# The router product taken from raw rows during the second layer's maxima, and the expert rows summed in the output tensor

## The chip, the cores and the metric

The kernel runs on one core of one Trainium2 chip. Its engines are PE (TensorE), DVE (VectorE), ACT (ScalarE), POOL (GpSimd) and SP (SyncE), each with its own instruction stream; they meet through semaphores. The metric is the device time of one execution, in microseconds (us), median of several runs; lower is better.

## What is computed

A graph layer of 1250 nodes with 768 features and 21,250 edges, to which a loop for each node is added. In short, with `ln` the layer norm without gain:

```
xn = ln(x)
x1 = x + GNN(xn) + MIX(xn)
GNN: two graph-attention layers (4 heads of 192, then 2 heads of 96, the softmax of each
     node over its edges is taken with the largest score subtracted), result out2 (1250 x 192);
     GNN = [xn, out2] @ Wu + bu
MIX: linear attention with 12 heads, projected
y = ln(x1)
probs = softmax(y @ router_w.T)          # 8 experts, the two most probable of each node are taken
out = x1 + sum over the 2 picks of balanced[t, e] * (silu(y @ w1[e].T) @ w2[e].T)
```

`balanced` divides a probability by a running importance of its expert, computed from the sum of `probs` over all nodes, and scales the two to a sum of one.

## The kernel before

Nodes lie in NT = 10 tiles of P = 128 rows (T = 1280 padded rows). Every engine's program is written out by hand, so its order is the order of the code, and `reserve`/`take`/`finished`/`evacuated` hand the 8 PSUM banks round in a list that all engines share. Before the second attention layer, `acc_d` in DRAM already holds x plus everything of x1 but the out2 part. The parts that matter here, in order of time:

- **First layer's aggregation** (`attention`, `aggregate`): DVE and ACT make one 128 x 1280 score tile per head and source tile, PE multiplies it (L1854). PE starts it after the small product of `b1T`.
- **Second layer's maxima.** PE spreads two columns to rows (`spread_row`, stage `aR`), then DVE runs 20 passes `masked_max` over 128 x 1280 (L1306), ten a head. After each head `leaky_max` gives `ucol`, and PE spreads it (stage `uR2`, L1615 with `ucol`), which ACT copies out (`rows_out`, L967). Only after both heads does ACT enter `attention` of layer 2.
- **Final projection and x1.** `fin_step(t)` on PE turns a tile of out2 and multiplies it by the lower part of Wu (`wuo`, two halves of 384 columns). `residual(t)` on DVE adds it to `x1` and takes the row statistics. SP writes each finished tile of x1 to `sum_d` in DRAM (L596).
- **Router.** For groups of 4, 4 and 2 tiles: `normalized` (DVE) makes y in `yrow`, `y_turned` (PE and ACT) turns it, `logits` (PE) multiplies it by the router weights `rw_raw` (8 columns). `shifted`, `exponentials` and `two_largest` give probabilities and picks, `ranks` (PE) counts places, `places` (DVE) computes the slot of each pick, and POOL scatters the token numbers into `list_d` (L711, two scatters a tile). SP writes y and its gated probabilities to `y_d` (L601).
- **Token lists.** POOL reads `list_d` back (L715). DVE takes from it the token of each of the 128 rows of NS = 27 expert tiles (L1575, 27 passes), into `token_ix`. Rows that no token fills get a padded row's number.
- **Experts** (27 tiles): POOL fetches rows of `y_d` (L721), PE turns them, multiplies by w1, turns, multiplies by w2, ACT and DVE scale by the gate into `yout`, and POOL adds the rows to `sum_d` with an accumulating scatter (L737). Each scatter waits until the one before has landed.
- **End.** When the last scatter has landed, SP copies `sum_d` to `out` in 10 DMAs (L605) and waits for them.

## Time and profile before

| | us |
|---|---|
| median of 3 runs (1143.0 to 1146.82) | 1143.82 |
| time of the profiled execution | 1147.77 |
| its span | 1145.8 |
| PE busy in the span | 958.8 (84%) |
| DVE busy | 679.7 (59%) |
| ACT busy | 404.4 (35%) |
| POOL busy | 406.6 (35%) |

The span runs from the first to the last record of the profiled execution; its own time has 2.0 us more around it. Busy times are averages over stages with different limits, so they don't say what a stage waits for. The chain that ended last is by engine 27% PE, 14% DMA, 12% DVE; its largest DMA piece is the scatter `sum_d<-yout` with 9% of the span.

### The profile page before, as it was taken

Reading aid. Unit: us, or ns where it says so; the run is one execution under the profiler, and the core shown is the slowest. Engines: PE = TensorE matmul, PEld = TensorE weight load, DVE = VectorE, ACT = ScalarE, POOL = GpSimd, SP = SyncE. Lnnn points to the kernel's source line nnn. Section 1 sums busy time; section 2 is a strip of 40 time slices with the busy share of each in tenths; the row PEclk is TensorE's granted clock in tenths of the full one; section 3 lists DMA queues with packets and bytes.
Section 4 is the critical chain, followed back from the end, with each engine's and each line's share of the span. In section 5 each row is a group of like instructions: output and inputs, shape, how many; then the busy total and the mean of one; then the engine's idle time right before and its main releaser. Section 6 shows DMA issues by size and latency. Waiting matters only on the chain.

```text
span 1145.8 us, 14465 instructions
## 1 busy us (share of the span) xinstructions
PE 958.8 (84%) x5152; PEld 815.6 (71%) x5152; DVE 679.7 (59%) x1687; ACT 404.4 (35%) x634; POOL 406.6 (35%) x321
## 2 busy tenths in 40 slices
PE   4999979999999949946999989358797749999991
PEld 3898648676979948946999989257765637767660
DVE  7679997104733215788888867969875362333330
ACT  2543010333320004455778855158421202222220
POOL 3168888888888820002000000000001243443431
PEclk9999997999999988986999989779796559999996
DMA  9986456422544591115000000340261424666556
GB/s 292 218 194 163 73 117 159 83 1 1 111 82 71 129 281 48 25 44 185 28 1 1 1 1 27 112 151 2 96 234 38 170 72 82 127 123 124 115 104 169
DMA packets 76370, 116.14 MB, mean 101 GB/s; under 512 B 33107, under 2 KB 51917, under 8 KB 76141
## 3 DMA queue, kind: packets, MB, share of 16 engines
q0 software_dynamic: 36128, 40.87, 21.2%
q1 hardware_dynamic: 40173, 74.36, 19.9%
q8 instruction: 42, 0.69, 0.2%
q14 instruction: 27, 0.22, 0.1%
HBM read 85.09 MB, written 33.96 MB: 104 GB/s over the span
## 4 chain that ended last, share of the span: by engine, by line
PE 27%; DMA 14%; DVE 12%; issue 5%; ACT 3%; POOL 2%; POOLq 0%; another core or an unknown queue 0%; DVEq 0%; ACTq 0%
PE bank L1615 15%; PE bank L1854 10%; DMA sum_d<-yout,sb_negq 9%; DVE sb_before L1306 5%; DVE pbuf L1361 3%; DMA cnt<-table 3%; DVE pbuf L1372 3%; DMA xs<-y_d,sb_negq 2%; PE bank L1626 2%; ACT h L974 1%; ACT vbuf L988 1%; POOL list_d L711 1%; DVE o L1402 1%; PE bank L1791 1%; ACT pbuf L997 0%
## 5 line engine op out<-in xcount | busy, mean ns | idle before, releaser
L655 POOL DMA_INDIRECT table<-match_n,slot_ix x168 | 278.6, 1658 | 92.9 <-issue 48.4
L1854 PE MATMUL bank<-h,pbuf 128*128 128x193 f32 (+1 forms) x1200 | 191.7, 323 | 20.3 <-DVE pbuf L1372 19.7
L1854 PEld LDWEIGHTS bank<-h,pbuf 128*128 128x128 f32 x1200 | 184.9, 200 | 27.0 <-DVE pbuf L1372 24.4
L711 POOL DMA_INDIRECT list_d<-sb_wk,sb_negq x20 | 19.8, 991 | 342.0 <-DVE sb_negq L1518 336.5
L1306 DVE CUSTOM_DVE_ANT_0 sb_before<-a_row,pen 128x1280 bf16<-128x1280 f32 x60 | 89.5, 1491 | 17.9 <-ACT pen L931 12.5
L1170 DVE SCALAR_TENSOR_TENSOR junk_k<-keyrow,key,sb_before 128x384 uint8<-128x384 f32 x168 | 93.0, 617 | 10.2 <-DMA keyrow<-key_d 9.1
L1615 PE MATMUL bank<-xnT_hi,w_hi 128*128 128x512 f32 (+1 forms) x216 | 85.5, 396 | 11.9 <-issue 8.1
L997 ACT ACTIVATE pbuf<-pbuf 128x1280 f32<-128x1280 f32 x60 | 76.7, 1278 | 42.7 <-DVE pbuf L1361 42.7
L1372 DVE SCALAR_TENSOR_TENSOR pbuf<-pbuf,cnt 128x1280 f32<-128x1280 f32 x60 | 88.8, 1486 | 0.0
L1615 PE MATMUL bank<-w_hi,xnT_hi 128*128 128x384 f32 x240 | 83.1, 346 | 0.0
L1615 PE MATMUL bank<-w_hi,xnT_lo 128*128 128x384 f32 x240 | 81.4, 339 | 0.0
L1615 PE MATMUL bank<-w_lo,xnT_hi 128*128 128x384 f32 x240 | 81.3, 339 | 0.0
L737 POOL DMA_INDIRECT sum_d<-yout,sb_negq x27 | 42.9, 1589 | 106.6 <-DMA sum_d<-yout,sb_negq 73.9
L1615 PE MATMUL bank<-xnT_lo,w_hi 128*128 128x512 f32 (+1 forms) x216 | 78.9, 365 | 0.0
L1615 PE MATMUL bank<-xnT_hi,w_lo 128*128 128x512 f32 (+1 forms) x216 | 78.5, 364 | 0.0
L1615 PE MATMUL bank<-w_all,xT 128*128 x324 | 76.5, 388 | 0.9 <-issue 0.9
L1615 PE MATMUL bank<-w_all,hT 128*128 x216 | 75.3, 492 | 1.5 <-DVE hT L1602 1.5
L1615 PEld LDWEIGHTS bank<-w_all,xT 128*128 128x128 f32 x324 | 63.1, 195 | 15.6 <-issue 1.3
L1361 DVE SCALAR_TENSOR_TENSOR pbuf<-u_row,sb_scol,vbuf 128x1280 f32<-128x1280 f32 x40 | 61.9, 1548 | 20.2 <-PE bank L1854 13.0
L819 ACT ACTIVATE kq<-bank,sb_kqb_c 128x512 f32<-128x512 f32 (+1 forms) x36 | 22.2, 618 | 122.5 <-PE bank L1615 111.1
L1615 PEld LDWEIGHTS bank<-xnT_hi,w_hi 128*128 128x128 f32 x216 | 41.8, 194 | 21.8 <-issue 15.7
L1615 PEld LDWEIGHTS bank<-w_all,hT 128*128 128x128 f32 x216 | 38.9, 190 | 25.4 <-issue 2.1
(303 smaller groups left out, 1798.2 us busy)
## 6 DMA issues: line engine op xcount, KB each, us to landing
keyrow<-key_d SPq DMA_DIRECT2D x28, 384.0 KB
cnt<-table POOLq DMA_DIRECT2D x20, 320.0 KB, 9.3
w_all<-in_w1T SPq DMA_DIRECT2D x8, 768.0 KB
w_all<-in_w2T SPq DMA_DIRECT2D x8, 768.0 KB
u_row<-m_d POOLq DMA_DIRECT2D x8, 640.0 KB, 6.5
w_raw<-in_kqvT SPq DMA_DIRECT2D x4, 1152.0 KB
y_d<-yrow SPq DMA_DIRECT2D x10, 388.0 KB
acc_d<-ubuf SPq DMA_DIRECT2D x20, 192.0 KB, 2.5
```

Source lines behind the costliest of these rows:

```text
L655: pool.indirect_dma_start(table[i], bass.IndirectOffsetOnAxis(ap=slot_ix[:, g:g + 1], axis=0), match_n[:, g:g + 1], None, compute_op=ALU.a ...
L711: pool.indirect_dma_start(list_d, bass.IndirectOffsetOnAxis(ap=place[0:n, k, t:t + 1], axis=0), token_no[0:n, t:t + 1], None, bounds_check ...
L737: pool.indirect_dma_start(sum_d, bass.IndirectOffsetOnAxis(ap=token_ix[:, s:s + 1], axis=0), yout[s % YO][:, :], None, compute_op=ALU.add, ...
L819: step(nc.scalar.activation(kq[j % 2][0][:, 0:w], b[:, 0:w], ACT.Identity, bias=kqb_c[:, col:col + 1]))
L997: nc.scalar.activation(pbuf[i % 3][:, :], pbuf[i % 3][:, :], ACT.Exp).then_inc(e_done, 1)
L1170: nc.vector.scalar_tensor_tensor(out=junk_k[g % 2][:, :], in0=keyrow[c % KR][:, w:w + KW * P], scalar=key[:, g:g + 1], in1=before[:, first ...
L1306: ins = nc.vector.tensor_tensor_reduce(out=junk_m[:, :], in0=rows_a[h][:, :], in1=pen_t[:, :], scale=1.0, scalar=-3e38, op0=ALU.subtract, ...
L1361: nc.vector.scalar_tensor_tensor(out=pbuf[i % 3][:, :], in0=u1_r[h][:, :], scalar=scol[:, h, st:st + 1], in1=vbuf[i % 2][:, :], op0=ALU.ad ...
L1372: nc.vector.scalar_tensor_tensor(out=pbuf[i % 3][:, :], in0=pbuf[i % 3][:, :], scalar=2.0, in1=cnt[st][:, :], op0=ALU.min, op1=ALU.mult).t ...
L1615: return nc.tensor.matmul(o, l, r, start=first, stop=last)
L1626: ins = nc.tensor.transpose(b[0:channels, j * P:(j + 1) * P], piece(j), ident[:, :])
L1854: ins = nc.tensor.matmul(b[:, d * stride:d * stride + chans + 1], score[:, dt * P:(dt + 1) * P], h_t[:, st, h, 0:chans + 1], start=st == 0 ...
```

## The change

- The router product is taken from x1 without normalizing first. With `rw_raw` centred (its column means over the 768 features subtracted, by DVE, from a column sum `csum` that PE makes before the first aggregation), the logits are x1 @ centred, times the row's inverse deviation. x1 is split in the part of `acc_d` and the out2 part: SP loads the ten raw tiles of `acc_d` into a ring of four (`xa`), PE turns and multiplies them, and likewise `wuo` (two pieces), in 12 items `PRE` that stand between `aR` and the second `uR2`. The out2 part is then two matmuls of 8 columns more in each `fin_step`. `y_turned` and `logits` are gone.
- `normalized` runs on ACT. The groups are 6 and 4 tiles.
- SP writes x1 straight to `out`, and POOL scatters into `out`, with indices of its own (`sum_ix`): `out` has no padded rows, so an unused row adds its zeros to a real row that no other row of that scatter names (the token that this partition has in the expert's first tile, or a `spare` one that didn't pick the expert). `sum_d` and the ten copies at the end are gone.

```diff
-        GROUPS = [range(4), range(4, 8), range(8, NT)]
...
+        GROUPS = [range(6), range(6, NT)]
...
+        PRE = [("x", t) for t in range(NT)] + [("w", j) for j in range(2)]
+        PRE_FIRST = 7
...
             finished(sp, "w2", NT - 1)
+            for t in range(NT):
+                if t >= XA:
+                    finished(sp, "preT", t - XA, 1)
+                sp.dma_start(xa[t % XA][:, :], acc_d[t * P:(t + 1) * P, :]).then_inc(xa_in[t % XA], 16)
...
-                sp.dma_start(sum_d[t * P:(t + 1) * P, :], x1[:, t, :]).then_inc(sum_begun, 16)
+                sp.dma_start(out[t * P:t * P + rows(t), :], x1[0:rows(t), t, :]).then_inc(sum_begun, 16)
...
+                    sp.wait_ge(y2_done, t + 1)
+                    sp.dma_start(y_d[t * P:(t + 1) * P, :], yrow[:, t, :]).then_inc(y_out, 16)
+            sp.wait_ge(sum_begun, 16 * NT)
             sp.wait_ge(sum_out, 16 * NS)
-            for t in range(NT):
-                r = slice(t * P, t * P + rows(t))
-                sp.dma_start(out[r, :], sum_d[r, :]).then_inc(out_sent, 16)
-            sp.wait_ge(out_sent, 16 * NT)
...
+            pool.wait_ge(sums_known, 1)
...
+                pool.indirect_dma_start(out, bass.IndirectOffsetOnAxis(ap=sum_ix[:, s:s + 1], axis=0),
                                         yout[s % YO][:, :], None, compute_op=ALU.add,
-                                        bounds_check=T + P - 1).then_inc(sum_out, 16)
+                                        bounds_check=N - 1).then_inc(sum_out, 16)
...
+            def normalized(g):
+                for t in GROUPS[g]:
+                    nc.scalar.activation(yrow[:, t, 0:D], x1[:, t, :], ACT.Identity, scale=rs2[:, t:t + 1],
+                                         bias=shift[:, t:t + 1]).then_inc(y2_done, 1)
...
+                        b = finished(dve, "csum")
+                        nc.vector.tensor_scalar(run[:, :], b[:, 0:E], -1.0 / D, None, ALU.mult).then_inc(free("csum"), 1)
+                        evacuated(dve, "csum")
+                        nc.vector.tensor_tensor(rw_raw[:, :, :], rw_raw[:, :, :], run[:, :].unsqueeze(1).broadcast_to([P, KD, E]),
+                                                ALU.add).then_inc(centred, 1)
...
+                    ins = nc.vector.tensor_tensor(a, a, b[:, 0:HALF], ALU.add)
+                    if hf == 0:
+                        evacuated(dve, "pre", t)
+                        ins = nc.vector.tensor_tensor(prob[:, t, :], b[:, HALF:HALF + E], before_att[:, t, :], ALU.add)
+                    ins.then_inc(free("fin", t, hf), 1)
...
             def shifted(g):
                 tl, n = span(g), len(GROUPS[g])
...
+                inv_std_end(rs2, span(g))
+                step(nc.vector.tensor_reduce(out=r10[:, tl], in_=prob[:, tl, :], op=ALU.max, axis=AX.X))
+                step(nc.vector.tensor_tensor(prob[:, tl, :], prob[:, tl, :], over_e(r10[:, tl]), ALU.subtract))
+                step(nc.vector.scalar_tensor_tensor(out=shift[:, tl], in0=mv3[:, tl, 0], scalar=-1.0, in1=rs2[:, tl],
+                                                    op0=ALU.mult, op1=ALU.mult))
+                nc.vector.tensor_tensor(prob[:, tl, :], prob[:, tl, :], over_e(rs2[:, tl]), ALU.mult).then_inc(shift_done, 1)
...
-            for t in range(4):
+            for t in GROUPS[0]:
                 residual(t)
             inv_std_begin(mv3, span(0))
-            residual(4)
-            normalized(0)
-            for t in range(5, 8):
-                residual(t)
+            residual(6)
+            shifted(0)
+            residual(7)
+            two_largest(0)
+            places(0)
+            residual(8), residual(9)
             inv_std_begin(mv3, span(1))
-            shifted(0)
-            residual(8)
-            two_largest(0)
-            normalized(1)
-            places(0)
-            residual(9)
-            inv_std_begin(mv3, span(2))
-            normalized(2)
             shifted(1)
             two_largest(1)
             places(1)
-            shifted(2)
-            two_largest(2)
-            places(2)
...
+            for e in range(E):
+                ins = nc.vector.tensor_scalar(matches[:, e, :], from_one, spare_at[:, e:e + 1], None, ALU.is_equal)
+            ins.then_inc(spare_found, 1)
...
+            heads_of = listed[:, 0:E * KT].rearrange("p (e k) -> p e k", k=KT)[:, :, 0]
+            nc.vector.tensor_copy(spare, finished(dve, "spare")[:, 0:E]).then_inc(free("spare"), 1)
+            evacuated(dve, "spare")
+            step(nc.vector.tensor_scalar(first_real, heads_of, float(T), None, ALU.is_lt))
+            step(nc.vector.tensor_tensor(firsts, heads_of, spare, ALU.subtract))
+            step(nc.vector.tensor_tensor(firsts, firsts, first_real, ALU.mult))
+            step(nc.vector.tensor_tensor(firsts, firsts, spare, ALU.add))
+            by_tile(firsts, others)
+            step(nc.vector.tensor_scalar(real, row_f, float(T), None, ALU.is_lt))
+            step(nc.vector.tensor_tensor(row_f, row_f, others, ALU.subtract))
+            step(nc.vector.tensor_tensor(row_f, row_f, real, ALU.mult))
+            nc.vector.tensor_tensor(sum_ix, row_f, others, ALU.add).then_inc(sums_known, 1)
...
+            pe.wait_ge(router_in, 16)
+            b = take(pe, "csum")
+            for k in range(KD):
+                ins = mm(b[:, 0:E], ones[:, :], rw_raw[:, k, :], k == 0, k == KD - 1)
+            ins.then_inc(full("csum"), 1)
...
+            def pre_turned(i):
+                kind, t = PRE[i]
+                if kind == "x":
+                    pe.wait_ge(xa_in[t % XA], 16 * (t // XA + 1))
+                for h in range(2):
+                    b = take(pe, "preT", i, h)
+                    for j in range(3):
+                        c = slice((3 * h + j) * P, (3 * h + j + 1) * P)
+                        if kind == "x":
+                            ins = nc.tensor.transpose(b[:, j * P:(j + 1) * P], xa[t % XA][:, c], ident[:, :])
+                        else:
+                            ins = nc.tensor.transpose(b[:, j * C2:(j + 1) * C2], wuo[:, t, c], ident[0:C2, 0:C2])
+                    ins.then_inc(full("preT", i, h), 1)
+
+            def pre_logits(i):
+                n = P if PRE[i][0] == "x" else C2
+                evacuated(pe, "preT", i, 0), evacuated(pe, "preT", i, 1)
+                b = take(pe, "pre", i)
+                for k in range(KD):
+                    ins = mm(b[0:n, 0:E], xp[i % 2][:, k, 0:n], rw_raw[:, k, :], k == 0, k == KD - 1)
+                ins.then_inc(full("pre", i), 1)
+
+            def spread_rows(h):
                 pe.wait_ge(m_done, H1 + 1 + h)
                 for k in range(2):
                     spread_row("uR2", (k,), h, ucol[:, h, k, :])
+
+            pe.wait_ge(centred, 1)
+            pe.wait_ge(g_in, 32)
+            pre_turned(0)
+            for i in range(len(PRE)):
+                if i + 1 < len(PRE):
+                    pre_turned(i + 1)
+                pre_logits(i)
+                if i == PRE_FIRST - 1:
+                    spread_rows(0)
+            spread_rows(1)
             aggregate("agg2", H1, H2, h2, S2, C2, 2, 5)
 
 
             evacuated_all(pe, "agg2")
-            pe.wait_ge(g_in, 32)
 
...
+                            evacuated(pe, "pre", len(PRE) - 1)
+                            for k in range(2):
+                                ins = mm(b[:, HALF:HALF + E], o2T[(t - 1) % 2][:, k, :], wuo_rw[:, k, :], k == 0, k == 1)
                         ins.then_inc(full("fin", t - 1, hf), 1)
...
+            for t in range(NT):
                 fin_step(t)
-            pe.wait_ge(router_in, 16)
-            logits(0)
-            fin_step(9)
-            pe.wait_ge(numbers_done, 12)
+            pe.wait_ge(numbers_done, 14)
             ranks(0)
-            fin_step(10)
-            logits(1), logits(2)
-            ranks(1), ranks(2)
-            pe.wait_ge(prob_done, 3)
...
+            pe.wait_ge(spare_found, 1)
+            b = take(pe, "spare")
+            for e in range(E):
+                ins = mm(b[:, e:e + 1], matches[:, e, :], slot_no[:, 0:1], True, True)
+            ins.then_inc(full("spare"), 1)
```

**PE, between the `aR` rows and the second layer's aggregation.** Before (`w2g` is the end of the layer's product, `scol` are the aR rows, `ucol` the uR2 rows, `h,pbuf` the aggregation):

```order
L1615 MATMUL bank<-w2g_lo,oT_152 128x192
L1615 MATMUL bank<-w2g_hi,oT_153 128x192
L1615 MATMUL bank<-sb_ident,sb_scol 128x128 x20
L1615 MATMUL bank<-sb_ident,ucol 128x128 x40
L1854 MATMUL bank<-h_154,pbuf_143 128x97 x10
L1854 MATMUL bank<-h_154,pbuf_144 128x97 x10
L1854 MATMUL bank<-h_154,pbuf_145 128x97 x10
```

With the change, from the seventh item's product on (ahead of it stand the turns of eight raw tiles, six transposes each, and six products; `xa` and `xp` are a raw tile before and after it is turned, `sb_rw_raw` the router weights):

```order
L1665 MATMUL bank<-sb_rw_raw,xp_185 128x8 x6
L1665 MATMUL bank<-sb_ident,ucol 128x128 x20
L1951 MATMUL bank<-sb_ident,xa_181 128x128 x6
L1665 MATMUL bank<-sb_rw_raw,xp_186 128x8 x6
L1951 MATMUL bank<-sb_ident,xa_182 128x128 x6
L1665 MATMUL bank<-sb_rw_raw,xp_185 128x8 x6
L1953 MATMUL bank<-sb_ident,wuo 128x96 x6
L1665 MATMUL bank<-sb_rw_raw,xp_186 128x8 x6
L1953 MATMUL bank<-sb_ident,wuo 128x96 x6
L1665 MATMUL bank<-sb_rw_raw,xp_185 96x8 x6
L1665 MATMUL bank<-sb_rw_raw,xp_186 96x8 x6
L1665 MATMUL bank<-sb_ident,ucol 128x128 x20
```

Twelve items have come between rows that stood together; the first 20 `ucol` rows stand behind seven of them, the second 20 behind all twelve.

**PE, at the end of the final projection.** Before, from the product of the eighth tile to that of the ninth:

```order
L1626 MATMUL bank<-sb_ident,o_161 96x128 x2
L1615 MATMUL bank<-wuo,o2T_164 128x384 x4
L1626 MATMUL bank<-sb_ident,yrow 128x128 x12
L1615 MATMUL bank<-sb_rw_raw,xT_169 128x8 x6
L1626 MATMUL bank<-sb_ident,yrow 128x128 x6
L1615 MATMUL bank<-sb_rw_raw,xT_170 128x8 x6
L1626 MATMUL bank<-sb_ident,yrow 128x128 x6
L1615 MATMUL bank<-sb_rw_raw,xT_169 128x8 x6
L1615 MATMUL bank<-sb_rw_raw,xT_170 128x8 x6
L1626 MATMUL bank<-sb_ident,o_161 96x128 x2
L1615 MATMUL bank<-wuo,o2T_163 128x384 x4
L1615 MATMUL bank<-sb_row_t,sb_wq 128x8
```

With the change:

```order
L1676 MATMUL bank<-sb_ident,o_161 96x128 x2
L1665 MATMUL bank<-wuo,o2T_163 128x384 x2
L1665 MATMUL bank<-sb_row_b,o2T_163 128x8 x2
L1665 MATMUL bank<-wuo,o2T_163 128x384 x2
L1665 MATMUL bank<-sb_row_t,sb_wq 128x8
L1665 MATMUL bank<-sb_row_t,sb_ones 128x8
L1665 MATMUL bank<-sb_row_t,sb_wq 128x8
L1665 MATMUL bank<-sb_row_t,sb_ones 128x8
```

The ninth tile follows the eighth, and the ranks (`sb_row_t`) come with no turned `yrow` and no `rw_raw` product ahead of them; each tile has two matmuls of 8 columns more.

**DVE, from the token passes to the first expert copies.** Before:

```order
L1575 SCALAR_TENSOR_TENSOR sb_row_b,sb_row_t<-sb_wq,sb_row_t,sb_negq 128x97 x3
L1578 CAST sb_negq<-sb_row_t 128x3
L1575 SCALAR_TENSOR_TENSOR sb_row_b,sb_row_t<-sb_wq,sb_row_t,sb_negq 128x97 x24
L1578 CAST sb_negq<-sb_row_t 128x24
L1595 COPY xT_169<-bank 128x384
L1595 COPY xT_170<-bank 128x384
L1584 ISA sb_row_b<-xs_171,sb_run 128x8
```

With the change (`sb_negq` at the end of it is `sum_ix`, and the two copies of `xT` follow right behind):

```order
L1612 SCALAR_TENSOR_TENSOR sb_row_b,sb_row_t<-sb_wq,sb_row_t,sb_negq 128x97 x24
L1615 CAST sb_negq<-sb_row_t 128x24
L1618 COPY sb_row_b<-bank 128x8
L1620 TENSOR_SCALAR sb_row_b<-sb_negq 128x8
L1621 TENSOR_TENSOR sb_row_b<-sb_negq,sb_row_b 128x8
L1622 TENSOR_TENSOR sb_row_b<-sb_row_b 128x8
L1623 TENSOR_TENSOR sb_row_b<-sb_row_b 128x8
L1581 TENSOR_TENSOR sb_accb<-sb_KD,sb_row_b 128x216
L1582 TENSOR_REDUCE sb_row_b<-sb_accb 128x27
L1625 TENSOR_SCALAR sb_row_b<-sb_row_t 128x27
L1626 TENSOR_TENSOR sb_row_t<-sb_row_t,sb_row_b 128x27
L1627 TENSOR_TENSOR sb_row_t<-sb_row_t,sb_row_b 128x27
```

Eleven operations have come between the 24 later token passes and the two copies.

## Rows read from the trace of the kernel before

**Rows 1.** Timeline of the SP queue: start us, us, engine, line, operation, out<-in, count.
```profile
712.09 5.73 SPq L569 DMA_DIRECT2D w_all<-in_w1T  x5
...
1130.79 6.37 SPq L605 DMA_DIRECT2D out<-sum_d  x10
```

**Rows 2.** Waits of the SP queue, last stretch: us in total, times, longest us.
```profile
SPq L59 <- DMA out<-sum_d: 8.2, 1, 8.2
```

**Rows 3.** Timeline of POOL (releaser of the idle time before in brackets): lists, first fetch.
```profile
883.70 1.07 POOL L711 DMA_INDIRECT list_d<-sb_wk,sb_negq  x1 [316.28 <-DVE sb_negq L1518]
...
928.23 0.97 POOL L711 DMA_INDIRECT list_d<-sb_wk,sb_negq  x1 [0.30 <-issue]
...
934.98 1.05 POOL L721 DMA_INDIRECT xs<-y_d,sb_negq  x1 [3.69 <-DVE sb_negq L1578]
```

**Rows 4.** Line L737, the scatter of expert rows: durations, first and last start, landing.
```profile
L737 POOL DMA_INDIRECT sum_d<-yout,sb_negq x27: 1551/1591/1645, 956.5 to 1125.8; - x27
...
DMA to landing us min/median/max: 5.0/5.5/6.1
```

**Rows 5.** Timeline of PE, layer 2: aR rows, then uR2 rows twice.
```profile
714.17 4.73 PE L1615 MATMUL bank<-sb_ident,sb_scol 128*128 128x128 f32 x40 [2.11 <-DVE sb_a L1427]
733.54 6.16 PE L1615 MATMUL bank<-sb_ident,ucol 128*128 128x128 f32 x40 [14.64 <-DVE ucol L1318]
749.71 6.59 PE L1615 MATMUL bank<-sb_ident,ucol 128*128 128x128 f32 x40 [10.01 <-DVE ucol L1318]
```

**Rows 6.** Timeline of PE, final projection, router product, ranks, first expert product.
```profile
853.13 2.75 PE L1615 MATMUL bank<-wuo,o2T 96*128 96x384 f32 x8
855.71 1.48 PE L1626 MATMUL bank<-sb_ident,yrow 128*128 128x128 f32 x12
857.26 1.48 PE L1615 MATMUL bank<-sb_rw_raw,xT 128*128 128x8 f32 x12
...
876.74 0.57 PE L1615 MATMUL bank<-sb_row_t,sb_wq 128*128 128x8 f32 x2 [6.37 <-issue]
...
899.49 2.84 PE L1626 MATMUL bank<-sb_ident,yrow 128*128 128x128 f32 x12
902.13 5.13 PE L1615 MATMUL bank<-sb_rw_raw,xT 128*128 128x8 f32 x24
...
943.55 7.72 PE L1615 MATMUL bank<-w_all,xT 128*128 x24 [0.92 <-issue]
```

**Rows 7.** Windows: stretch, its us, busy us of each engine, PE clock, DMA.
```profile
717.00:725.00 8.00, 1.90 (x18) 1.71 (x16) 7.49 (x10) 1.60 (x4) 0.00 (x0) 0.87 1.10 351
840.00:850.00 10.00, 10.00 (x36) 5.92 (x35) 8.54 (x22) 2.63 (x5) 0.00 (x0) 1.00 0.75 296
856.00:861.00 5.00, 4.93 (x45) 4.72 (x44) 4.18 (x10) 2.51 (x6) 0.00 (x0) 1.00 0.39 157
861.00:865.00 4.00, 4.00 (x30) 3.93 (x28) 0.10 (x1) 2.25 (x4) 0.00 (x0) 0.73 0.00 0
899.00:904.00 5.00, 5.00 (x25) 4.82 (x25) 3.44 (x19) 2.19 (x5) 0.00 (x0) 0.50 0.00 0
```

**Rows 8.** Timeline of DVE: places(0), two_largest(1), the copies before the first expert product.
```profile
880.33 0.46 DVE L1506 TENSOR_TENSOR sb_accb<-bank,sb_wq 128x288 f32<-128x288 f32 x1 [0.33 <-PE bank L1615]
...
882.65 0.17 DVE L1518 CAST sb_negq<-sb_row_b 128x8 uint32<-128x8 f32 x1
...
900.39 0.19 DVE L1472 TENSOR_REDUCE sb_r<-sb_prob 128x4 f32<-128x32 f32 x1 [0.30 <-ACT sb_prob L1051]
...
904.54 0.19 DVE L1496 TENSOR_TENSOR yrow<-sb_prob,sb_row_t 128x32 f32<-128x32 f32 x1
...
942.80 1.01 DVE L1595 COPY xT<-bank 128x384 f32<-128x384 f32 x2
```

**Rows 9.** Timeline of PE, start of the first layer's aggregation.
```profile
524.77 2.72 PE L1615 MATMUL bank<-sb_ones,sb_row_b 1*96 1x1 f32 x16 [1.24 <-DVE sb_row_b L1410]
529.09 31.19 PE L1854 MATMUL bank<-h,pbuf 128*128 128x193 f32 x170 [1.61 <-DVE pbuf L1372]
```

167 lines of the change are left out of this document (83 added, 84 removed).

## The prediction

> **What bounds the kernel now.** I read the end of the program first, then went back along whatever released it. In the timeline of the SP queue [rows 1] the reader sees the ten copies to `out` issued from 1130.79 us on, over 6.37 us, and in the waits of SP [rows 2] another 8.2 us until they have landed: 14.6 us in which no engine computes. They start when the last of 27 accumulating scatters has landed; the row on that scatter [rows 4] has the first starting at 956.5 and the last at 1125.8, one every 6.51 us, with 5.5 us from issue to landing. So scatters, each waiting for the one before, set the pace of the experts. Ahead of them stand the token lists. POOL's timeline [rows 3] shows the first list scatter at 883.70, the last at 928.23 (0.97 busy behind 0.30 of idle time that nothing but issue ended, so 1.3 us each where they queue), then the first fetch at 934.98. PE waits for that chain; before it PE itself is what the router waits for, with turns and products of 8 columns [rows 6]. In the second layer's maxima the roles are reversed: PE sits idle behind DVE between its three sets of rows (714.17, 733.54, 749.71) [rows 5].
>
> **The change part by part**, against the profiled execution (span 1145.8, its own time 1147.8).
>
> *The end.* The copies go and nothing takes their place: 14.6 us gained. Each scatter moves the same rows as before, only into `out`; I take its 5.5 us as unchanged [rows 4] (bounds below). The writes of x1 to `out` are issued where those to `sum_d` were, far ahead of the first scatter.
>
> *Router path.* Before, PE turned and multiplied every tile of y behind the final projection. With the change only the projection is left, and I work out when the last placement is known, in the time scale of the trace before:
> - One projection tile costs 2.8 us: eight instructions of 384 columns take 2.75 [rows 6], and in the window 840 to 850 PE is busy throughout, DVE for 8.54 of 10 us [rows 7]. The two matmuls of 8 columns are 4 instructions more; 12 such took 1.48 us [rows 6], so 0.5 us, and the tile costs some 3.25. DVE gets one small operation of 0.2 and stays just below. The product at 853.13 is the eighth tile's, so the seventh ended at about 852.9; seven times 0.45 later is 856.1.
> - DVE then ends that tile's sums and statistics (858.3), nine small steps of 0.2 (860.2), the eighth tile meanwhile (862.9), and 22 steps of `two_largest`, which took 4.3 us for 4 tiles (900.39 to 904.54 and its own length) [rows 8] and take about 5 for 6: 867.9.
> - PE ranks six tiles in 12 matmuls. After idle time a pair of instructions takes 0.57 with its own latency, and in a row 0.43 each (24 instructions in 5.13) [rows 6]: 5.4 us, 873.3. `places` took 2.5 us for 4 tiles (880.33 to 882.65 and the cast) [rows 8], 3.4 for 6 with two steps added: 876.8. Tiles 9 and 10 follow in DVE, 5.3 us: 882.1.
> - Square root, `shifted` and exponential 2.8 (884.9), `two_largest` 4.4 (889.3), ranks of 4 tiles 4.6 (893.9), `places` 2.7 (896.6). POOL starts 0.9 later (883.70 behind the cast of 882.65 and its 0.17) [rows 3, 8], and its eighth scatter, at 1.3 us each, starts at 906.6 instead of 928.23. Group 0's 12 scatters (15.5 us from 877.7) are done by then. Gain 21.7 us; the first fetch moves from 934.98 to 913.3.
>
> *Index arithmetic.* The first expert product (943.55) follows the DVE copies of 942.80 [rows 6, 8]. Eleven operations now stand ahead of these copies: nine small ones at 0.2 and two over 27 x 8 elements at about 0.4, less overlap: 2.9 us lost. The router path is worth 18.8 us net. What I cost at nothing (the durations estimated from like rows): `matches` and the `spare` product (8 DVE operations, some 2 us, and 8 matmuls, 3.4 us) lie under POOL's last eight scatters (10 us); if those were gone they would cost up to 5 us. `normalized` on ACT (10 x 0.9 us) lies beside DVE. SP's last two expert loads and ten y copies (5.4 MB) start at about 881, and at the 296 GB/s of the window 840 to 850 [rows 7] take 18 us: 899 at the earliest, 14 us ahead of the fetch that waits for them.
>
> *First layer.* PE makes `csum` behind the 2.72 us of `b1T` and then idled 1.61 before the aggregation at 529.09 [rows 9]. Twelve instructions at half clock are 2.57 us (24 in 5.13 at 902.13 [rows 6]), so 1.0 us shows. DVE adds two small steps with two score tiles in hand: nothing. Loss 1.0.
>
> *Maxima of layer 2.* Here is the cost. PE gets 12 items, each with 6 turns and 6 products of 8 columns, between 718.9 (end of the aR rows at 714.17, 4.73 long) and the second ucol rows, which started at 749.71 [rows 5]; ACT is queued behind them with layer 2's attention, and SP behind PE's fifth to sixth item with five loads of w1, three tiles of x1 and four loads of w2, needed only after 830 us. The raw tiles come in time: their loads start where SP now starts w1 (712.09) [rows 1], 0.4 MB each. At the full clock an item is 0.74 + 1.48 (half of 1.48, and 1.48 [rows 6]), call it 2.1 back to back; at half clock 1.4 + 2.57 = 3.9. Full, the first seven end at 735, just behind DVE's first head, and all is done before 749.7: no loss, and ucol rows that start at 2.4 GHz take 4.5 instead of 6.6 us: a gain of 2. Half, the twelve items take until 767 with the first ucol rows among them, and these rows themselves 6.5 us: about 18 us lost.
> What the clock does with this mix the trace shows once: after the projection the same turns and products run with a granted clock of 1.00 in 856 to 861, and it falls in 861 to 865 (0.73) although PE is busy for all 4.00 us; in 899 to 904 they run at 0.50, PE busy 5.00 of 5 [rows 7]. (With PE idle from 718.9 it fell before 725: 0.87 in 717 to 725.) So the level of 2.4 GHz lasts some 7 us in this mix and then goes to 1.2, and long rows of 128 columns bring it back: the 40 instructions at 733.54 took 6.16, those of 714.17 4.73 [rows 5]. I take that: from 718.9 seven us do three items, four at 3.9 plus the eighth turn end at 743, the first ucol rows at 749; seven us do three more, the last two (narrower) end at 761, the second ucol rows at 767.6 against 756.3. Loss 11.3 us.
> The Trainium skill (TensorE: Matmul & The Clock Gate, Part 4: PE-mode transpose) says that the full clock does not engage for transpose mode, since transposes don't count as busy in the same way. This speaks against the change: by it alone the items would lose some 18 us here instead of 11. By that rule, the trace agrees in that the 12 turns at 899.49 stayed at 0.50.
>
> **Sum.** -14.6 - 18.8 + 1.0 + 11.3 = -21.1: 1126.7 for an execution like the profiled one, and from the median, 4.0 lower, 1143.8 - 21.1 = 1122.7. The runs shown spread by 0.3%, about what a measurement of this kernel can tell from no change.
>
> **The rivals.**
> 1. *The clock stays up in the maxima.* For: PE is now busy without a gap from the aR rows on. Against: it fell at 861 to 865 with PE busy. 1143.8 - 14.6 - 18.8 + 1.0 - 2 = 1109.4.
> 2. *Half clock nearly throughout.* For: the stretch of 899 to 904 at 0.50 with PE busy. Against: ucol rows raised it before. 1143.8 - 32.4 + 18 = 1129.4. The rule of the Trainium skill above is the same case seen from its side.
> 3. *Slower than before: the scatters into `out`.* Unused rows used to hit a block of padded rows of their own; now they read and write real rows spread over the tensor. Landing time is the pace of the loop, so each extra 0.1 us costs 2.7. Above 6.3 us instead of 5.5 (27 x 0.8 = 21.6) the change loses; at 6.4 the time is 1122.7 + 24.3 = 1147.0. Landings reach 6.1 already [rows 4]. Against: same rows, same bytes, same queue; the rows of real tokens were always spread. Below, a gain is capped: PE is busy nearly all of the loop, 6.3 us a tile. So 2 to 3 us each way at equal odds, not more.
> 4. *The lists come no earlier*, because something else ends last, say the y copies at three times my 18 us. Then half of 18.8 stays away: 1132. The 14 us of slack speak against it.
>
> **How the numbers follow.** Forecast 0.52, rival 1 0.22, rival 2 0.18, rival 3 0.04, rival 4 0.04. The router path is a long sum of small steps, good to 4 us; with the clock's bounds the range is 1109 to 1131, and leaves out rivals 3 and 4 and half of what lies below rival 1. Faster by over 0.3% 0.95, within 0.3% 0.01, slower 0.04.
>
> **What would show it.** SP's row with the copies to `out` gone and the span ending within 1 us of the last landing; scatters still at 5.5 us and 6.5 apart; the first fetch 21 to 22 us earlier relative to the start of the projection, the first expert scatter 19; the granted clock between the two sets of ucol rows at 1.0, then 0.5, and the second set ending 9 to 13 us later than 756. I am wrong if that set starts at 750, if landings exceed 6 us, or if the first fetch waits for y rather than for the lists.

## The result and the profile after

| | before | after |
|---|---|---|
| median of its runs, us | 1144.78 (4 runs, 1143.0 to 1146.82) | 1130.36 (4 runs, 1127.45 to 1137.15) |
| ratio, 95% interval | | 0.9884 [0.9846, 0.9922] |
| profiled execution: time, span | 1147.77, 1145.8 | 1127.45, 1125.7 |
| PE busy in the span | 958.8 | 974.6 |
| DVE busy | 679.7 | 674.3 |

By the ratio the change is 13 us faster, not 21. It is faster by more than 0.3%, as forecast, but the median is 7.7 us above the predicted one, inside the range. The spans of the profiled pair differ by 20.1 us, close to the forecast, and that is luck: this is the fastest of the four executions. Its end gave 4.8 us less than forecast and its router 3.0 less, while the maxima cost 2.3 less and stretches that the forecast left at nothing ran 4.6 shorter.

The page of the changed kernel shows the chain that ended last with the same parts as before (PE 27%, DMA 15%, DVE 11%). The places that the prediction named come next, each in the view in which it stood before.

The timeline of PE in the changed kernel, from the aR rows to the second ucol rows, answers [rows 5]:

```profile
711.86 6.36 PE L1665 MATMUL bank<-sb_ident,sb_scol 128*128 128x128 f32 x40 [2.11 <-DVE sb_a L1468]
718.06 1.47 PE L1951 MATMUL bank<-sb_ident,xa 128*128 128x128 f32 x12
...
722.84 0.85 PE L1951 MATMUL bank<-sb_ident,xa 128*128 128x128 f32 x6
...
724.78 0.85 PE L1951 MATMUL bank<-sb_ident,xa 128*128 128x128 f32 x6
725.48 1.40 PE L1665 MATMUL bank<-sb_rw_raw,xp 128*128 128x8 f32 x12
...
731.62 2.57 PE L1665 MATMUL bank<-sb_rw_raw,xp 128*128 128x8 f32 x12
734.04 1.52 PE L1951 MATMUL bank<-sb_ident,xa 128*128 128x128 f32 x6
735.36 2.57 PE L1665 MATMUL bank<-sb_rw_raw,xp 128*128 128x8 f32 x12
737.77 6.04 PE L1665 MATMUL bank<-sb_ident,ucol 128*128 128x128 f32 x40
743.65 0.82 PE L1951 MATMUL bank<-sb_ident,xa 128*128 128x128 f32 x6
...
755.84 7.20 PE L1665 MATMUL bank<-sb_ident,ucol 128*128 128x128 f32 x40
```

and its windows (stretch, its us, busy us of each engine, PE clock, DMA) answer [rows 7]:

```profile
720.00:727.00 7.00, 7.00 (x66) 7.00 (x66) 6.83 (x11) 3.46 (x11) 0.00 (x0) 0.99 0.71 228
727.00:738.00 11.00, 11.00 (x55) 11.00 (x54) 10.64 (x17) 3.44 (x10) 0.00 (x0) 0.50 0.92 304
743.00:748.00 5.00, 5.00 (x47) 5.00 (x46) 4.81 (x9) 2.99 (x9) 0.00 (x0) 0.94 0.00 1
748.00:756.00 8.00, 8.00 (x49) 8.00 (x48) 0.17 (x1) 2.00 (x6) 0.00 (x0) 0.50 0.91 306
```

The reader is to see twelve items where PE stood idle for 14.64 and 10.01 us before, at two speeds: an item is six turns and twelve instructions of 8 columns, 0.85 and 1.40 us long at a clock of 0.99 (724.78 is 1.94 behind 722.84), and 1.52 and 2.57 at 0.50 (735.36 is 3.74 behind 731.62), with PE busy for the whole of both stretches. The second ucol rows end at 763.0 instead of 756.3 [rows 5]; counted from the start of the aR rows, which came 2.3 us earlier, that is 9.0 later.

The timeline of POOL in the changed kernel, for [rows 3], and the row on the scatter, for [rows 4]:

```profile
885.55 1.07 POOL L724 DMA_INDIRECT list_d<-sb_wk,sb_negq  x1 [321.02 <-DVE sb_negq L1561]
...
915.32 0.98 POOL L724 DMA_INDIRECT list_d<-sb_wk,sb_negq  x1 [0.31 <-issue]
...
922.21 1.06 POOL L734 DMA_INDIRECT xs<-y_d,sb_negq  x1 [3.80 <-DVE sb_negq L1615]
...
946.68 1.65 POOL L751 DMA_INDIRECT out<-yout,sb_negq  x1 [9.77 <-DVE yout L1659]
```

```profile
L751 POOL DMA_INDIRECT out<-yout,sb_negq x27: 1552/1588/1646, 946.7 to 1115.5; - x27
...
DMA to landing us min/median/max: 5.3/5.5/6.0
```

The last list scatter comes 12.9 us earlier on the clock of the trace, and since the projection itself begins 6.0 us later (836.22 against 830.24), 18.9 earlier in relation to it. Scatters last and land as before. The first fetch is 18.8 us earlier in the same relation, where 21 to 22 were forecast, and the first expert scatter 15.8, where 19 was.

At the end, the rows of the program's last line in the changed kernel (duration in ns, first start in us), and the waits of the SP queue:

```profile
L59 DVEq DRAIN  x1: 655/655/655, 1110.3 to 1110.3; - x1
L59 POOLq DRAIN  x1: 10222/10222/10222, 1115.3 to 1115.3; - x1
...
L59 SPq DRAIN  x1: 7/7/7, 1121.1 to 1121.1; - x1
```

```profile
SPq L59 <- PEq L59: 4.6, 1, 4.6
```

The copies are gone, but SP, done at 1121, then waits 4.6 us (the wait is put down to PEq, whose last work was long past). What it waits for stands in the first of these views: DRAIN, an instruction that each engine runs at the end of the program, takes 10.2 us on POOL and starts when the last scatter is issued, at 1115.3, while DVE's takes 0.66. It ends at 1125.5, and the program with it. The same row stood in the trace before, where nobody waited for it:

```profile
L59 POOLq DRAIN  x1: 10222/10222/10222, 1125.5 to 1125.5; - x1
L59 SPq DRAIN  x1: 7/7/7, 1145.6 to 1145.6; - x1
```

There it ended at 1135.7, under the copies that ran until 1145.4.

### The profile page after: what moved, and what is told of

The parts are those of the page before. It is cut to its first block, busy times and chain, and to the rows that moved or that the text cites. A ratio compares the mean times of both kernels' runs of the same rounds, so it can differ in the third digit from the quotient of the medians.

```text
span 1125.7 us, 14698 instructions
## 1 busy us (share of the span) xinstructions
PE 974.6 (87%) x5256; PEld 831.3 (74%) x5256; DVE 674.3 (60%) x1681; ACT 417.4 (37%) x658; POOL 408.6 (36%) x322
## 3 DMA queue, kind: packets, MB, share of 16 engines
q0 software_dynamic: 36048, 40.48, 21.7%
## 4 chain that ended last, share of the span: by engine, by line
PE 27%; DMA 15%; DVE 11%; issue 6%; ACT 3%; POOL 2%; another core or an unknown queue 1%; POOLq 0%; DVEq 0%; ACTq 0%
PE bank L1665 15%; DMA out<-yout,sb_negq 13%; PE bank L1904 9%; DVE pbuf L1408 3%; DVE pbuf L1397 3%; DVE sb_before L1342 2%; DMA cnt<-table 2%; PE bank L1676 1%; ACT h L988 1%; PE bank L1951 1%; ACT vbuf L1002 1%; POOL cnt L684 1%; DVE o L1443 1%; PE bank L1841 1%
## 5 line engine op out<-in xcount | busy, mean ns | idle before, releaser
L1904 PE MATMUL bank<-h,pbuf 128*128 128x193 f32 (+1 forms) x1200 | 189.8, 320 | 19.5 <-DVE pbuf L1408 18.9
L1011 ACT ACTIVATE pbuf<-pbuf 128x1280 f32<-128x1280 f32 x60 | 76.7, 1278 | 42.4 <-DVE pbuf L1397 42.4
L751 POOL DMA_INDIRECT out<-yout,sb_negq x27 | 42.9, 1589 | 105.8 <-DMA out<-yout,sb_negq 88.3
L833 ACT ACTIVATE kq<-bank,sb_kqb_c 128x512 f32<-128x512 f32 (+1 forms) x36 | 22.2, 618 | 123.3 <-PE bank L1665 103.2
L1665 PEld LDWEIGHTS bank<-xnT_hi,w_hi 128*128 128x128 f32 x216 | 42.2, 195 | 20.7 <-issue 14.5
L940 ACT ACTIVATE h<-bank,sb_rs 128x384 f32<-128x384 f32 x20 | 11.6, 582 | 122.3 <-PE bank L1665 122.3
```

What stands on the lines that cost most here:

```text
L751: pool.indirect_dma_start(out, bass.IndirectOffsetOnAxis(ap=sum_ix[:, s:s + 1], axis=0), yout[s % YO][:, :], None, compute_op=ALU.add, bou ...
L833: step(nc.scalar.activation(kq[j % 2][0][:, 0:w], b[:, 0:w], ACT.Identity, bias=kqb_c[:, col:col + 1]))
L940: nc.scalar.activation(h1[:, t, 2 * hf:2 * hf + 2, 0:C1], b[:, 0:HALF].rearrange("p (h c) -> p h c", h=2), ACT.Copy, scale=rs2[:, t:t + 1] ...
L1011: nc.scalar.activation(pbuf[i % 3][:, :], pbuf[i % 3][:, :], ACT.Exp).then_inc(e_done, 1)
L1665: return nc.tensor.matmul(o, l, r, start=first, stop=last)
L1904: ins = nc.tensor.matmul(b[:, d * stride:d * stride + chans + 1], score[:, dt * P:(dt + 1) * P], h_t[:, st, h, 0:chans + 1], start=st == 0 ...
```

## The experiments

Fifteen runs follow: eight edited kernels, and the change and the kernel before several times more. They fall in four groups, and all of a group ran on one chip beside the kernel before (its medians: 1145.2, 1147.9, 1146.2 and 1144.9; the third group has single executions alone). A ratio is that to the kernel before in the same group. Each profiled execution was also read stage by stage. The table gives, for each trace, the lengths in us of the stretches between nine points. PE's first row behind the reading of the count table starts the first; then come: start of the first aggregation, start of the aR rows of layer 2, start of its attention (ACT's first row there), start of the projection, first fetch of rows for an expert, first expert scatter, last expert scatter, end of the span. The first column is where the first point stood. The four traces of the change are after, again, change_third and change_fourth.

| trace | begins | to aggregation | to aR rows | maxima | attention | router, lists | to scatter | scatters | end | span |
|---|---|---|---|---|---|---|---|---|---|---|
| before | 431.3 | 97.8 | 185.1 | 42.5 | 73.6 | 104.7 | 21.5 | 169.3 | 20.1 | 1145.8 |
| before_again | 434.9 | 97.8 | 185.1 | 42.5 | 73.6 | 104.0 | 21.9 | 170.5 | 20.2 | 1150.3 |
| before_third | 432.3 | 98.1 | 180.3 | 44.1 | 73.6 | 100.7 | 21.8 | 170.8 | 21.4 | 1143.2 |
| after | 428.4 | 98.8 | 184.7 | 51.5 | 72.8 | 86.0 | 24.5 | 168.8 | 10.2 | 1125.7 |
| again | 429.8 | 98.0 | 187.4 | 54.8 | 72.8 | 84.4 | 23.5 | 171.6 | 10.2 | 1132.5 |
| change_third | 431.7 | 99.0 | 184.8 | 51.5 | 72.7 | 92.8 | 24.6 | 173.4 | 10.5 | 1141.0 |
| change_fourth | 428.4 | 97.9 | 190.6 | 54.8 | 72.8 | 84.6 | 23.5 | 172.6 | 10.4 | 1135.5 |
| router_only | 434.3 | 97.9 | 187.3 | 54.8 | 72.8 | 84.4 | 22.2 | 171.3 | 20.6 | 1145.5 |
| router_only_again | 429.3 | 98.8 | 184.7 | 51.5 | 72.9 | 84.2 | 22.3 | 171.2 | 20.5 | 1135.3 |
| out_only | 431.4 | 96.9 | 184.6 | 44.3 | 72.8 | 105.3 | 23.5 | 173.9 | 10.4 | 1142.9 |
| out_only_again | 430.2 | 97.6 | 185.0 | 42.4 | 73.5 | 100.9 | 24.8 | 172.7 | 10.4 | 1137.5 |
| drain_wait | 432.2 | 97.8 | 193.8 | 51.5 | 72.8 | 84.4 | 23.6 | 170.6 | 14.5 | 1141.2 |
| sums_late | 433.3 | 98.7 | 184.7 | 51.5 | 72.8 | 85.7 | 21.6 | 172.3 | 10.8 | 1131.5 |
| wide | 431.4 | 99.1 | 184.9 | 42.6 | 73.3 | 83.7 | 24.9 | 172.6 | 10.5 | 1122.9 |
| wide_late | 435.3 | 98.1 | 184.3 | 44.2 | 72.9 | 85.9 | 21.6 | 173.8 | 10.5 | 1126.5 |
| joined | 435.9 | 99.1 | 184.8 | 51.5 | 72.7 | 80.0 | 24.2 | 173.9 | 10.4 | 1132.5 |
| joined_wide | 431.9 | 98.6 | 184.6 | 42.6 | 71.1 | 79.9 | 24.4 | 175.8 | 10.4 | 1119.2 |

**The change again.** No edit.

> The changed kernel once more, unedited, for a closer ratio and a second trace. Theory A (what the first trace of it shows): the end gives only 9.8 us of the 14.6 forecast, because POOL's drain of 10.2 us behind the last scatter was hidden under the copies; the maxima lose 9 to 15 us, depending on where the clock level changes fall. Ratio 0.985 to 0.992 against the kernel before; the span ends 10.2 us after the start of the last scatter; the second ucol rows end 6 to 14 us later than before, relative to the end of layer 2's product. Theory B (the end was worth 14.6 and the first trace of the change was odd there): the span ends within 6 us of the last scatter's start.

Measured: 1133.66 (6 runs), ratio 0.9903 [0.9877, 0.9929]. The smaller gain repeats, and four of the six runs lie between 1131.77 and 1134.24.

**Router part alone.** The change with the sums back in a tensor of their own:

```
-   sp.dma_start(out[t * P:t * P + rows(t), :], x1[0:rows(t), t, :])
+   sp.dma_start(sum_d[t * P:(t + 1) * P, :], x1[:, t, :])
...
+   for t in range(NT):
+       sp.dma_start(out[r, :], sum_d[r, :]).then_inc(out_sent, 16)
```

and without `spare`, `matches` and the index arithmetic.

> The change without its second half: x1 and the scatters go to the internal tensor again, the ten copies to the output are back, the eleven index operations on DVE and the spare product are gone. Theory A: loses the 9.8 us at the end, wins back the 2.9 of index arithmetic, so it is about 7 us slower than the change as a whole, and about 6 us faster than the kernel before. Theory B (the end was worth 14.6): 11 to 12 us slower than the change, within 3 us of the kernel before.

Measured: 1144.4 (12 runs, 1136.91 to 1148.99), ratio 0.9987 [0.9965, 1.0009], 10.7 us above the change. That is far less of a gain than the 6 us that I had expected, and the times alone would fit theory B as well; the end stretch rules it out, 20.6 us here against 10.2 with the change. The table shows where it went in the traced execution: the router stage is 20.3 us shorter, but the maxima 12.3 longer, and three stretches that the edit doesn't touch are another 7 longer. The second trace tests whether these 7 belong to the edit.

> The router part alone, a second trace. Its first was 1145.5: router path 20 us shorter, maxima 12.3 longer, and 7 us more in stretches that the edit doesn't touch (table 3.0, clock behind the first aggregation 2.2, expert loop 2.1). Theory 1 (those 7 us are execution to execution): most of them gone, or in other places, and a span of 1136 to 1145. Theory 2 (the edit brings them): the same three stretches longer again, 1145.

Measured: span 1135.3, theory 1: two of the three stretches are back (the loop is not), the maxima 3.3 shorter. The same kernel lies 8 to 15 us below the three traces of before once, and among them the other time. So single executions differ by more than this part gives.

**GpSimd waits for its last scatter before it ends.**

```
+   pool.wait_ge(sum_out, 16 * NS)
```

> The change, with one more wait: POOL waits for the last scatter to land before its program ends. If POOL's drain is a fixed 10.2 us from POOL's last instruction, it starts about 5 us later and the time grows by 5 us. If the drain waits for the DMA itself and then does little, the drain shrinks to some 5 us and the time stays.

Measured: 1137.89 (10 runs), ratio 0.9942 [0.9909, 0.9975], 4.2 us above the change in the same group; the two intervals overlap, so the trace has to tell. The last line's rows in it:

```profile
L59 POOLq DRAIN  x1: 8360/8360/8360, 1132.6 to 1132.6; - x1
```

```profile
SPq L59 <- PEq L59: 8.5, 1, 8.5
```

Started only when the last scatter had landed, at 1132.6 instead of 1126.7, the DRAIN took 8.4 us, and SP waited 8.5. So it is not a wait for that scatter: at least 8.4 us of it are left when the scatter has landed. It starts when POOL has nothing left to issue, and the end of the program waits for it. What it does in this time no trace shows.

**Exchanged operands in the maxima.** In the router product of the raw rows the router's weights become the stationary operand and the turned tile streams, so each instruction has 128 moving columns instead of 8. The result, 8 x 128, is turned back.

```
-   ins = mm(b[0:n, 0:E], xp[i % 2][:, k, 0:n], rw_raw[:, k, :], k == 0, k == KD - 1)
+   ins = mm(b[0:E, 0:P], rw_raw[:, k, :], xp[i % 2][:, k, 0:n], k == 0, k == KD - 1)
...
+   nc.tensor.transpose(b[:, 0:E], lg8[i % 2][:, :], ident[0:E, 0:E])
```

> The change with the operands of the raw tiles' router product exchanged: the router weights (8 columns) are loaded, the turned tile of 128 columns streams through, and a small transpose turns the 8 x 128 result back (one instruction more an item). At a given clock the product takes the same time. Theory A (the products of 8 columns are what lets the clock fall): the granted clock stays at 1.0 between the aR rows and the second ucol rows, each item takes 2.1 to 2.3 us, the second ucol rows start when DVE ends its maxima, and the time is 9 to 14 us below the change. Rival (transposes alone let the clock fall, whatever the product): the clock falls as before and the time is within 3 us of the change.

Measured: 1124.8 (6 runs), ratio 0.9818 [0.9786, 0.985]: 8.9 us below the change in the same group, though it has ten small turns more. PE in this kernel's trace:

```profile
715.38 4.73 PE L1674 MATMUL bank<-sb_ident,sb_scol 128*128 128x128 f32 x40 [2.11 <-DVE sb_a L1477]
719.95 1.47 PE L1960 MATMUL bank<-sb_ident,xa 128*128 128x128 f32 x12
...
728.38 1.48 PE L1674 MATMUL bank<-xp,sb_rw_raw 128*8 128x128 f32 x12
729.79 0.22 PE L1979 MATMUL bank<-sb_ident,lg 8*128 8x8 f32 x1
729.94 0.87 PE L1960 MATMUL bank<-sb_ident,xa 128*128 128x128 f32 x6
730.75 1.48 PE L1674 MATMUL bank<-xp,sb_rw_raw 128*8 128x128 f32 x12
...
737.03 4.73 PE L1674 MATMUL bank<-sb_ident,ucol 128*128 128x128 f32 x40
...
751.35 6.25 PE L1674 MATMUL bank<-sb_ident,ucol 128*128 128x128 f32 x40
```

```profile
715.38:725.00 9.62, 9.60 (x82) 8.45 (x82) 6.28 (x9) 5.62 (x13) 0.00 (x0) 1.00 0.66 225
725.00:735.00 10.00, 10.00 (x82) 7.53 (x81) 9.64 (x17) 5.15 (x18) 0.00 (x0) 1.00 0.64 206
735.00:745.00 10.00, 10.00 (x86) 8.60 (x85) 9.79 (x13) 5.75 (x16) 0.00 (x0) 1.00 1.04 338
```

An item now takes 2.37 us (728.38 to 730.75), at a granted clock of 1.00 for 30 us, with PE just as busy as in the change. The maxima stage is back at 42.6 us, what it was with no items at all. A product of 128 columns costs the same 1.48 us for twelve instructions as one of 8, and what it gives is that the clock stays up. The turns are untouched and were as many: they alone are not what lowers it in this mix. So the sum's largest loss was the price not of the work, but of its shape. The Trainium skill (TensorE: Matmul & The Clock Gate, Part 4: PE-mode transpose) says that the full clock doesn't engage for transpose mode; this trace differs: six turns took 0.87 us at 1.00 here and 1.52 at 0.50 in the change, and the measurement decides. No run has a long stretch of turns without products between them.

**The kernel before, twice more.**

> The kernel before, unedited, for a second trace. In its first trace the stretch from the first aggregation to the aR rows of layer 2 took 185.1 us, in the changed kernels' traces 184.7, 184.9, 187.3, 187.4 and 193.8; the stretch from the first to the last expert scatter took 169.3 us before and 168.8, 170.6, 171.3, 171.6, 172.6 after. Theory 1 (both stretches vary from one execution to the next, whatever the kernel): this trace differs from 185.1 or from 169.3 by more than 1 us. Theory 2 (the change itself lengthens them): this trace repeats 185.1 and 169.3 within 0.5 us. The maxima stage (start of the aR rows to the start of layer 2's attention) repeats 42.5 us under both.

> The kernel before, a third trace, read stage by stage against the others. The traces so far show the granted clock of 1.0 coming back behind the first aggregation after three different times: in one group the stretch from the first aggregation to the aR rows of layer 2 takes 184.3 to 185.1 us (before twice, the change, its late sums, both exchanged-operand kernels, scatters alone), in a second 187.3 to 187.4 (the change again, router part alone), in one 193.8 (GpSimd waiting). Theory 1 (which of them comes is drawn anew in each execution, whatever the kernel): the kernel before can show any of them, and its stretches of 42.5 us in the maxima and 169 to 171 in the expert loop stay. Theory 2 (the change brings the later ones): 184 to 185.5 again.

Measured: spans 1150.3 and 1143.2. The stretch to the aR rows was 185.1 and 180.3, the router 104.0 and 100.7, the scatters 170.5 and 170.8: theory 1 in both, by 1.3 us in the scatters of the one and 4.8 ahead of the aR rows in the other. The maxima of the third trace took 44.1 us where both theories had 42.5: the granted clock was at 0.50 for 3.4 us of its aR rows, which took 6.36 us instead of 4.73. The kernel before varies too.

**Scatters into the output alone.** The kernel before, with the scatters, `spare` and the index arithmetic of the change:

```
-   pool.indirect_dma_start(sum_d, bass.IndirectOffsetOnAxis(ap=token_ix[:, s:s + 1], axis=0),
+   pool.indirect_dma_start(out, bass.IndirectOffsetOnAxis(ap=sum_ix[:, s:s + 1], axis=0),
```

> The kernel before with the scatters into the output and the index arithmetic alone: router, groups and maxima as before. By the theory of the end-of-program drain on GpSimd (10.2 us behind the last scatter, hidden under the copies before): 9.8 us gained at the end, 2.0 to 3.0 lost to the index arithmetic ahead of the first expert copies, so 6.8 to 7.8 us faster than before, 1137.5. By the prediction (all 14.6 us of the copies gained): 11.7 us faster, 1133.5. The drain row again 10.2 us long, started with the last scatter. Router: first fetch 104 to 105 us behind the start of the projection, as before. If scatters into the output lengthen the loop, first to last scatter above 171 us while the kernel before stays at 169.

> The scatters into the output alone, a second trace. Its first was 1142.9 with an expert loop of 173.9 us and a maxima stage of 44.3, against 169.3 to 170.5 and 42.5 before, and its twelve times were 1139.6 to 1150.8. Theory 1 (the longer loop comes from the destination): loop 173 to 175 again. Theory 2 (it is execution to execution): 169 to 172. End 10.2 to 10.8 us, fetch to first scatter 23.5, both by the drain theory.

Measured: 1144.93 (12 runs, 1139.58 to 1150.84), ratio 0.9966 [0.9943, 0.9989], and a second span of 1137.5. Both traces show the end at 10.4 us, as by the drain, and the way to the first scatter 1.7 to 3.0 us longer than the mean of before, by the index arithmetic. Its rows in the first:

```profile
L59 POOLq DRAIN  x1: 10362/10362/10362, 1132.3 to 1132.3; - x1
```

The gain in time is 3 to 4 us, where the drain theory gave 7. What took the rest is seen in part: the scatters took 173.9 and 172.7 us, and over all traces the stretch is 169.3 to 171.3 where they go to `sum_d` (5 traces, mean 170.6) and 168.8 to 175.8 where they go to `out` (12 traces, mean 172.7). That is 2 us, or 0.08 for each scatter, in the direction of the third rival, with single traces that overlap; the median time to landing is 5.5 to 5.6 us in the former and 5.5 to 5.7 in the latter. It isn't shown that the destination is the cause.

**Index arithmetic later.** The eleven operations behind the turned copies and gates of the first two tiles:

```
+   turned(0), turned(1)
+   gates(0), gates(1)
    heads_of = listed[:, 0:E * KT].rearrange("p (e k) -> p e k", k=KT)[:, :, 0]
...
-   turned(0), turned(1)
-   gates(0), gates(1)
```

> The change with the index arithmetic on VectorE behind the turned copies and gates of the first two expert tiles, still ahead of the first scatter. Theory 1 (the eleven operations ahead of the copies delay the first expert product by their length): first fetch to first scatter back from 23.5 to 24.5 us to about 21.5 to 22, 2 to 3 us faster than the change, 1131. Theory 2 (what they delay is off the path, since the first scatter waits for its indices too): same as the change, 1133.7, within 1 us.

Measured: 1132.7 (6 runs), ratio 0.9869 [0.9835, 0.9902]. The first scatter did come at 21.6 us behind the fetch instead of 23.5 to 24.6, as theory 1 had it. The gain in time can't be told: the interval overlaps with the change's own. With the exchanged operands as well:

> The exchanged operands (128 moving columns in the router product) together with the late index arithmetic. The exchange alone was 1124.8, 9 us below the change in the same call; its maxima stage 42.6 us instead of 51.5 to 54.8, at a granted clock of 1.00 nearly throughout. If both effects add: 1122, maxima stage 42 to 44 us again. If the clock's staying up was chance, the maxima stage is 51 to 55 us and the time 1131.

Measured: 1126.62 (6 runs), ratio 0.9806 [0.9779, 0.9832], no better than the exchange alone (0.9818). The maxima stage was short again (44.2), so that wasn't chance. Whether the loop also ends earlier can't be told: from first fetch to last scatter the four traces of the change took 193.3, 195.1, 198.0 and 196.1 us and late sums 193.8; with the exchanged operands it was 197.5, and 195.4 with late sums added.

**The change a third time.**

> The change, a third trace. Its maxima stage took 51.5 us once and 54.8 once, against 42.5 before. Theory 1 (the stage's length follows from when the clock comes back further up, drawn anew in each execution): 51.5 if the stretch ahead of it takes 184.7 or 193.8 us, 54.8 if it takes 187.4. Theory 2 (it is independent of it): any pairing. Start of the projection to the first fetch 84.4 to 86.0 us (103.9 to 105.3 without the router part), last scatter to the end 10.2 to 10.8, expert loop 169 to 173.

Measured: span 1141.0, time 1142.69. Maxima 51.5 behind 184.8, theory 1 (the fourth trace then had 54.8 behind 190.6, which is neither of the pairs named). New is the router stage of 92.8 us. PE in this trace, from the start of the projection:

```profile
840.69 2.93 PE L1665 MATMUL bank<-wuo,o2T 96*128 96x384 f32 x4
843.41 0.86 PE L1665 MATMUL bank<-sb_row_b,o2T 96*128 96x8 f32 x4
...
860.05 2.77 PE L1665 MATMUL bank<-wuo,o2T 96*128 96x384 f32 x4
...
866.45 1.84 PE L1665 MATMUL bank<-wuo,o2T 96*128 96x384 f32 x4
868.13 0.51 PE L1665 MATMUL bank<-sb_row_b,o2T 96*128 96x8 f32 x4
```

A tile is 6.4 us at half the clock and 3.25 at the full one, and the full one came back only at about 867, 27 us after the start: the granted clock was at 0.50 for 27.3 us. In the nine other traces with 8-column products in the projection it was there for 10.2 us, in all five of before and of the scatters alone for 6.8. Windows of four us behind the start of the projection (836.22 in the first trace of after, 830.24 before) show it:

```profile
840.22:844.22 4.00, 4.00 (x12) 2.64 (x11) 1.01 (x3) 0.03 (x1) 0.00 (x0) 0.50 1.10 352
844.22:848.22 4.00, 4.00 (x13) 2.25 (x13) 2.03 (x6) 0.35 (x1) 0.00 (x0) 0.73 1.05 393
```

```profile
834.24:838.24 4.00, 4.00 (x13) 2.28 (x12) 2.34 (x5) 0.38 (x1) 0.00 (x0) 0.84 1.09 351
838.24:842.24 4.00, 4.00 (x16) 2.40 (x15) 3.16 (x7) 0.50 (x2) 0.00 (x0) 1.00 1.05 395
```

The change puts four instructions of 8 columns into every tile of the projection. The last experiment takes them out.

**Joined projection.** The attention's share of the router product lies as eight columns more beside the second half of the projection's weights, so that the same instructions, of 392 columns instead of 384, make both.

```
-   wuo = at("wuo", SL[1] + 12288, [C2, 2, D])
+   wuo = at("wuo", SL[1] + 12288, [C2, 2, D + E])
...
-   ins = mm(b[:, 0:HALF], o2T[(t - 1) % 2][:, k, :], wuo[:, k, hf * HALF:(hf + 1) * HALF], k == 0, k == 1)
...
-   ins = mm(b[:, HALF:HALF + E], o2T[(t - 1) % 2][:, k, :], wuo_rw[:, k, :], k == 0, k == 1)
+   n = HALF + hf * E
+   ins = mm(b[:, 0:n], o2T[(t - 1) % 2][:, k, :], wuo[:, k, hf * HALF:hf * HALF + n], k == 0, k == 1)
```

> The change, unedited, beside the two below. By its earlier runs 0.985 to 0.992 of the kernel before; clock back 8 to 10 us after the start of the projection or much later, start of the projection to first fetch 84.4 to 86.0 us (92.8 in one trace).

> The change with the attention's share of the router product made by the same instructions as the projection: 392 columns instead of 384 in the second half of each tile, and no product of 8 columns there. Theory 1 (the 8-column products hold the clock down in the projection): clock back after 4 to 5 us as in the kernel before, tiles 2.8 to 2.9 us apart instead of 3.25, so the first fetch 3 (seven tiles by 0.4) plus about 3 (two tiles at the half clock) = 6 us earlier than the change: start of the projection to first fetch 78 to 80. Time 6 us below the change. Theory 2 (the clock's return has nothing to do with them): tiles 2.85 apart but the clock back after 8 to 10 us again, gain 3 us alone, 82. The maxima stage is unchanged (51.5 or 54.8).

> The joined projection and the exchanged operands in the maxima together. Under theory 1, 9 + 6 = 15 us below the change, 1118; under theory 2, 12 us, 1121. Maxima stage 42.5 to 44.2 us, clock 1.00 throughout.

Measured: the change 1133.31 (12 runs, 1130.91 to 1145.38), ratio 0.9912 [0.9886, 0.9939]; joined 1130.01 (5 runs), 0.9866 [0.9848, 0.9883]; joined with exchanged operands 1118.66 (5 runs, 1114.56 to 1121.05), 0.9766 [0.9744, 0.9789]. PE in the trace of joined:

```profile
844.96 5.54 PE L1665 MATMUL bank<-wuo,o2T 96*128 96x384 f32 x8
850.73 2.96 PE L1665 MATMUL bank<-wuo,o2T 96*128 96x384 f32 x8
853.74 2.77 PE L1665 MATMUL bank<-wuo,o2T 96*128 96x384 f32 x8
856.57 2.77 PE L1665 MATMUL bank<-wuo,o2T 96*128 96x384 f32 x8
```

The half clock now lasts 6.8 us, in this trace and in that of joined with exchanged operands. It costs one tile (5.54), and the later ones are 2.83 us apart; start of the projection to first fetch is 80.0 and 79.9 us, where 78 to 80 was expected under theory 1 and 82 under theory 2. So the 8-column products were what held the clock down in the projection, though it came back 7.1 us after the start and not 4 to 5. Joined alone gained 3.3 us in the median where 6 was expected (by the ratios 5; the intervals only just fail to overlap, and its scatters took 173.9); both edits together gained 14.7 of 15. This last kernel leaves nothing out, and is 26 us faster than before and 12 below the lowest median of the change.

## Why the prediction was right and wrong

The means of the traces, three of before and four of the change, give a sum to hold against the forecast's:

| stretch | forecast | measured | |
|---|---|---|---|
| end | -14.6 | -10.2 | wrong: a drain of 10.2 us comes out from under the copies |
| router and lists | -21.7 | -16.2 | oversized: -18.2 without the third trace; the clock comes late in the projection |
| index arithmetic | +2.9 | +2.3 | right |
| first layer, `csum` | +1.0 | +0.5 | right |
| maxima | +11.3 | +10.1 | right: 9.0 or 12.3 against the usual 42.5 |
| attention of layer 2 | 0 | -0.8 | not in the forecast |
| scatters | 0 | +1.4 | within the 2 to 3 us named for rival 3 |
| to the aR rows | 0 | +3.4 | not touched by the change: when the clock comes back |
| up to the first point | 0 | -3.2 | not touched by the change |
| sum | -21.1 | -12.8 | medians: -14.4 at first, -11.6 in two later groups |

**The end.** The step that failed most plainly is "The copies go and nothing takes their place: 14.6 us gained". Something did: POOL's DRAIN, 10.2 us from the last scatter. The forecast end was 20.05 - 14.6 = 5.5 us, the landing; it is 10.2 to 10.8 in every kernel without the copies, 14.5 when the DRAIN starts late. The row was in the trace before, at 1125.5 and 10.2 us long. I had gone back along what released the last instruction, and a row that releases nothing isn't on that way. What would have found it is the question of what else ends after the point to which the end moves. The sign that I had named, a span ending within 1 us of the last landing, was the right one to look for: it ended 4.8 later.

**Router.** The step-by-step time scale was sound (ranks, places, scatters, tile pitch of 3.25), and a usual trace of the change is at 84.4 to 86.0 us. In the first trace, told in the time scale of before, the ranks began at 870.0 instead of 867.9 and the last list scatter at 909.3 instead of 906.6. Two things were missing. The window 840 to 850 from which I took 2.8 us for a tile has the clock at 1.00; the first tiles in the change run at 0.50 for twice as long after the start as before (10.2 us against 5.3), since the 8-column products are now among them: the second product starts 6.57 us behind the first and the third 4.47 behind the second in the first trace, and in one trace of four the first four are 6.4 to 6.6 apart. joined put this right and got 5 us back. And the stage of before was itself 104.7, 104.0 and 100.7 in three traces: one trace gave the forecast no measure of that.

**Maxima.** "The level of 2.4 GHz lasts some 7 us in this mix and then goes to 1.2" held: in after it fell at about 727, 9 us after the first item, came back during the first ucol rows and lasted until 748. The second set ended 6.7 us later than before, and the stage was 9.0 and 12.3 us longer. Rival 1, the clock that stays up, was a property of the product's shape, which I took as given; wide shows it at no loss, 42.6 us. Rival 2, half clock nearly throughout, didn't occur, and its 18 us don't follow from the prediction's own terms: twelve items of 3.9 us and ucol rows of 6.5 from 718.9 on end at 772, 22 us behind 749.7. Rival 3's price is small, 2 us on average of the 22 it needed. Rival 4 didn't occur: y copies were issued by 900 and the fetch followed the lists at 922.

**The spread.** That one kernel runs from 1131 to 1145 us is in part the clock as well. The stretch to the aR rows took 180.3, 184 to 185, 187.4, 190.6 or 193.8 us. In the last third of this stretch the granted clock is at 0.50 not at all (before_third), for 6.8 us (before), 13.7 (again), 20.5 (change_fourth) or 27.3 us (drain_wait), at the same work, and the stretch grows with it, by 13.5 us from the first to the last. The windows at the half clock in before and in drain_wait:

```profile
675.10:681.90 6.80, 6.80 (x35) 6.73 (x34) 3.07 (x17) 2.41 (x9) 0.00 (x0) 0.50 0.01 2
```

```profile
674.00:701.30 27.30, 27.10 (x129) 26.84 (x129) 12.71 (x64) 9.23 (x34) 0.00 (x0) 0.50 0.00 1
```

The Trainium skill (TensorE: Matmul & The Clock Gate, Part 1) says that the amount of work done before the full clock is granted differs from run to run of one kernel, because the chip's observation of the engine isn't tied to the program's start. The traces agree: before alone showed 185.1, 185.1 and 180.3. Whether the change makes the late returns more frequent is open; of five traces without the router part none is above 185.1, and of twelve with it four are. All that the change puts ahead of these stretches is `csum`.

**What stays open**: the sum of the parts. The ratios of the two parts (0.9987 and 0.9966) give some 5 us together, and the change 11 to 14. Their second traces, spans of 1135.3 and 1137.5 against a mean of 1146.4 before, would give 20. I read it as the same spread, but it isn't shown.

## What to carry to other kernels

When a tail is removed, list everything that ends between its start and its end, waited for or not: the longest of these is the new end. Price PE work that fills idle time by its shape too: where, as here, a product has 8 moving columns and 128 stationary ones, exchange the operands or hang the few columns on a wide product next to it, and look at the granted clock before and after. And take more than one trace of a kernel whose stages lie where the clock changes, or the size of a term will be that of one execution.

## What the runs showed of the hardware

- POOL's DRAIN at the end took 8.4 us when its scatters had landed and 10.2 to 10.8 when the last had just been issued, against 0.6 to 2.5 us on DVE, ACT and PE and 0.007 on SP.
- Twelve instructions with 128 moving and 8 stationary columns took 1.48 us at the full clock, as many with 8 moving and 128 stationary 1.40 to 1.48. In the maxima the granted clock stayed at 1.00 for 30 us with items of the first kind and fell to 0.50 after 9 with items of the second, both with PE busy without a gap.
- In the projection, with four 8-column instructions to every eight of 384 columns, the granted clock was at 0.50 for 10.2 us in nine traces and 27.3 in one; with wide instructions alone (384 or 392 columns) it was 6.8 us in all seven.
